# Row-count pairs in the score items, and four TensorE steps moved within the slot, in an attention and expert kernel

## The reference, cut to what matters

```
xn  = layernorm(x)                                  # no scale, no shift
q, k, v = xn Wq^T + bq, xn Wk^T + bk, xn Wv^T + bv  # 16 heads of 8
attn    = softmax(causal(q k^T / sqrt(8))) v  Wo^T + bo
logits  = xn gate^T                                 # 8 experts
moe     = sum over the best 2 experts of softmax(top 2 logits) * (xn We[e])
out     = x + attn + moe
```

## Time and profile before

| | |
|---|---|
| median of three runs | 512.64 us |
| the profiled execution's own time | 513.41 us |
| its span, first to last instruction | 511.3 us |
| PE busy (TensorE matmul) | 476.1 us, 93% |
| DVE busy (VectorE) | 420.2 us, 82% |
| ACT busy (ScalarE) | 395.3 us, 77% |
| POOL busy (GpSimd) | 346.7 us, 68% |
| mean granted TensorE clock | 0.98 of full speed |

### The profile page before, as it was taken

How to read it: one execution, slowest core, us unless ns; L and a number is a source line. 1 busy time by engine, 2 the same in 40 slices (tenths; PEclk the granted TensorE clock), 3 DMA queues, 4 the chain that set the end, 5 groups by cost and what they waited for, 6 DMA issues and landing times.

```text
span 511.3 us, 17283 instructions
## 1 busy us (share of the span) xinstructions
PE 476.1 (93%) x6242; PEld 390.2 (76%) x6242; DVE 420.2 (82%) x1144; ACT 395.3 (77%) x1063; POOL 346.7 (68%) x561
## 2 busy tenths in 40 slices
PE   2548799999999999999999999999999999999985
PEld 1426588888888888888888888888888888888863
DVE  5898688888888988888888988888888988887721
ACT  3545578888888888888888888888888888887773
POOL 7264747777777777777777777777777777755443
PEclk9967989999999999999999999999999999999998
DMA  4755755556555666655555565655555566551000
GB/s 124 193 141 121 182 122 149 148 136 148 134 139 140 145 164 151 146 144 143 133 140 140 144 163 144 157 142 144 135 135 140 143 163 152 131 140 38 14 13 22
DMA packets 64345, 67.78 MB, mean 133 GB/s; under 512 B 7916, under 2 KB 59244, under 8 KB 59548
## 3 DMA queue, kind: packets, MB, share of 16 engines
q1 hardware_dynamic: 64260, 66.68, 52.5%
HBM read 44.90 MB, written 21.23 MB: 129 GB/s over the span
## 4 chain that ended last, share of the span: by engine, by line
PE 85%; issue 4%; DMA 3%; POOL 3%; ACT 2%; DVE 2%; SPq 0%; POOLq 0%; DVEq 0%; ACTq 0%
PE m L856 22%; PE oT_ps L926 17%; PE scoreT_ps L902 12%; PE score_ps L882 11%; PE scoreT_ps L907 5%; PE score_ps L876 5%; PE m L968 3%; PE m L1011 3%; PE m L1029 3%; PE m L941 2%; PE m L1036 1%; DMA scratch<-parts 1%; DMA qstack<-mT 1%; ACT probs L502 1%; POOL parts L374 1%
## 5 line engine op out<-in xcount | busy, mean ns | idle before, releaser
L630 DVE TENSOR_REDUCE negmax<-score_ps 128x2 f32<-128x512 f32 (+1 forms) x384 | 250.6, 680 | 56.7 <-PE score_ps L882 52.7
L502 ACT ACTIVATE probs<-scoreT_ps 128x512 f32<-128x512 f32 x384 | 216.8, 603 | 75.5 <-PE scoreT_ps L902 48.0
L397 POOL TENSOR_TENSOR fours<-lower,upper 128x512 f32<-128x512 f32 x64 | 81.7, 1276 | 54.0 <-ACT upper L552 54.0
L856 PE MATMUL m<-we_hl,xnT_hl 128*128 128x512 f32 x384 | 113.6, 417 | 0.0
L882 PE MATMUL score_ps<-kstack,qstack 72*128 72x128 bf16 (+1 forms) x1024 | 103.4, 223 | 6.0 <-DVE negmax L630 5.8
L902 PE MATMUL scoreT_ps<-qstack,kstack 123*128 123x128 bf16 (+1 forms) x1024 | 101.8, 221 | 4.2 <-DMA qstack<-mT 3.5
L926 PE MATMUL oT_ps<-probs,vaug 128*32 128x256 f32 (+1 forms) x2048 | 97.3, 330 | 0.2 <-ACT probs L502 0.2
L902 PEld LDWEIGHTS scoreT_ps<-qstack,kstack 123*128 123x128 bf16 (+1 forms) x1024 | 67.9, 98 | 27.3 <-ACT probs L502 15.3
L926 PEld LDWEIGHTS oT_ps<-probs,vaug 128*32 128x32 f32 x2048 | 57.4, 110 | 29.3 <-ACT probs L502 0.4
L552 ACT ACTIVATE upper<-m,weight 128x128 f32<-128x128 f32 x256 | 73.3, 377 | 8.1 <-PE m L856 8.1
L882 PEld LDWEIGHTS score_ps<-kstack,qstack 72*128 72x128 bf16 (+1 forms) x1024 | 71.9, 100 | 9.1 <-DVE negmax L630 8.6
(11 more groups left out here) (84 smaller groups left out, 641.0 us busy)
## 6 DMA issues: line engine op xcount, KB each, us to landing
kstack<-scratch SPq DMA_DIRECT2D x93, 192.0 KB
scratch<-parts SPq DMA_DIRECT2D x64, 192.0 KB, 2.3
qstack<-scratch SPq DMA_DIRECT2D x62, 192.0 KB
qstack<-scratch SPq DMA_DIRECT2D x31, 256.0 KB
x_sb<-in_x SPq DMA_DIRECT2D x32, 128.0 KB, 2.3
scratch<-parts SPq DMA_DIRECT2D x32, 128.0 KB, 1.9
out<-out_sb SPq DMA_DIRECT2D x32, 128.0 KB, 2.9
kstack<-scratch SPq DMA_DIRECT2D x6, 96.0 KB
```

What stands on the lines that cost most here:

```text
L397: g.tensor_tensor(fours[:, :, q, :], lower[:, :, q, :], upper[:, :, q, :], ALU.add).then_inc(pool_sum, 1)
L502: a.activation(o, i, ACT.Exp, scale=SCALE).then_inc(act_exp, 1)
L630: v.tensor_reduce(o, score_ps[n % 2][:].rearrange("p (h k) -> p h k", h=w), axis=AX.X, op=ALU.max, negate=True).then_inc(dve_max, 1)
L856: ins = tn.matmul(o, l, r, start=first, stop=l is low)
```

## The change

The results are the same, and the number of matmuls, copies and reductions is the same.

- **Row-count pairs.** Within a score item of 72 and 123 rows, and a transposed one of 123 and 74, the two matmuls with few rows are issued first, then the two with 123.
- **Maxima.** Their transpose goes behind the projection in step 1 and into `oT_ps` rather than m0; the products with the values of step 3 wait for the copy `mT`.
- **Expert product 2** (the third of four) moves from step 9 to step 8, right behind the turned attention output. VectorE's `o_sb` moves ahead of the maximum of step 9.
- **Normalised values** are turned in step 11 rather than 10, behind the turned input. The copy `oTn` on ScalarE follows it.
- **Output product** with Wo, VectorE's `out_sb` and the store move to step 1 of the next slot.

```diff
@@ score_item
-                    for c in range(2):
-                        h = head(grp, 2 * (j - 1) + c)
-                        for q, top in ((0, MAX_ROW), (1, ALL_ROWS)):
+                    for q, top in ((0, MAX_ROW), (1, ALL_ROWS)):
+                        for c in range(2):
+                            h = head(grp, 2 * (j - 1) + c)
                             ins = tn.matmul(ps[:, c * S + q * P:c * S + (q + 1) * P], qs[0:top, h, P:S],
@@ scoreT_item
-                    for c in range(2):
-                        h = head(grp, 2 * j + c)
-                        for q, top in ((0, ALL_ROWS), (1, MAX_ROW + MAX_PARTS)):
+                    for q, top in ((1, MAX_ROW + MAX_PARTS), (0, ALL_ROWS)):
+                        for c in range(2):
+                            h = head(grp, 2 * j + c)
@@ TensorE, slot
+                    if n == 1 and has(s, -3):
+                        give_output(t + (-3))
...
+                    if n == 1 and has(s, PRE):
+                        pe.wait_ge(act_upper, upto(fin, per=2))
+                        project(pre)
                     if n == 1 and has(s, -1):
                         pe.wait_ge(dve_split, upto(mix, per=2))
-                        pe.wait_ge(dve_out, upto(fin + (-1)))
-                        tn.transpose(m0[:, 0:P // 2].bitcast(BF16), ...
-                    if n == 1 and has(s, PRE):
-                        pe.wait_ge(act_upper, upto(fin, per=2))
-                        project(pre)
+                        pe.wait_ge(act_oT, upto(fin + (-1)))
+                        tn.transpose(oT_ps[:, 0:P // 2].bitcast(BF16), ...
                     if n == 3 and has(s, -2):
+                        if has(s, -1):
+                            pe.wait_ge(act_mT, upto(mix))
                         values(fin, 0)
                         values(fin, 1)
...
                     if n == 8 and has(s, -2):
                         pe.wait_ge(act_oT, upto(fin))
-                        if has(s, -1):
-                            pe.wait_ge(act_mT, upto(mix))
-                        else:
-                            pe.wait_ge(dve_out, upto(fin + (-1)))
+                        pe.wait_ge(dve_out, upto(fin + (-1)))
...
-                    if n == 9 and has(s, -1):
+                    if n == 8 and has(s, -1):
                         pe.wait_ge(dve_lower, upto(mix, per=2, k=1))
                         experts(mix, 2)
...
                         turn_input(t + NXT)
+                    if n == 11 and has(s, -2):
+                        pe.wait_ge(dve_o, upto(fin))
+                        for q in range(QT):
+                            ins = tn.transpose(m0[:, q * P:(q + 1) * P], o_sb[:, q, :], ident[:])
+                        ins.then_inc(pe_oTn, 1)
                     if n == 11 and has(s, -1):
                         pe.wait_ge(act_upper, upto(mix, per=2, k=1))
                         experts(mix, 3)
@@ VectorE, slot
                     if n == 1 and has(s, NXT):
                         measure(t + NXT)
+                    if n == 1 and has(s, -3):
+                        add_output(t + (-3))
...
                         ins.then_inc(dve_den, 1)
-                    if n == 9 and has(s, -2):
-
                         dve.wait_ge(dve_den, upto(fin))
                         dve.wait_ge(pe_oTn, upto(fin + (-1)))
@@ ScalarE, slot
                     if n == 11 and has(s, NXT):
                         copy_input(t + NXT)
+                    if n == 11 and has(s, -2):
+                        act.wait_ge(pe_oTn, upto(fin))
+                        act.wait_ge(pe_y, upto(fin + (-1)))
+                        a.copy(oTn[:], m0[:, 0:S]).then_inc(act_oTn, 1)
```

More of the change, by code:

```diff
@@ L313, in slot @@
             def slot(t, s):
-                if has(s, -3):
-                    store(t + (-3))
                 if has(s, -1):
@@ L323, in slot @@
                     load_stacks(Seq(0, PRE), slice(0, H), dma_stack[PRE])
+                if has(s, -3):
+                    store(t + (-3))
                 if has(s, NB):
@@ L563, in slot @@
                         act.wait_ge(dma_max, upto(mix + (-1), unit=16))
-                        a.copy(mT[:], m0[0:MAX_PARTS * QT * H, 0:P // 2].bitcast(BF16)).then_inc(act_mT, 1)
+                        a.copy(mT[:], oT_ps[0:MAX_PARTS * QT * H, 0:P // 2].bitcast(BF16)).then_inc(act_mT, 1)
                     if n == 2 and has(s, PRE):
@@ L592, in slot @@
                         upper_experts(mix, 0)
[L593 to L596, removed]
             act.wait_ge(pool_const, 2)
@@ L725, in fill_stack, with add_output @@
                               steps[HALF:P].unsqueeze(1).to_broadcast([HALF, H * QT, P])).then_inc(dve_stack, 1)
+            def add_output(m):
+                dve.wait_ge(pe_y, upto(m))
+                dve.wait_ge(pool_sum, upto(m, per=RESULT))
+                dve.wait_ge(dma_out, upto(m + (-1), unit=16))
+                v.tensor_tensor(out_sb[:].rearrange("p q d -> p (q d)"), m0[:, 0:S],
+                                res[:].rearrange("p q d -> p (q d)"), ALU.add).then_inc(dve_out, 1)
             def take_rest(pre):
@@ L782, in slot @@
                         split_max(t)
[L783 to L788, removed]
+                    if n == 11 and s == NSEQ + 1:
+                        add_output(fin)
             def first_normalised(nxt):
@@ L951, in project, with give_output @@
                 ins.then_inc(pe_qk, 1)
+            def give_output(m):
+                pe.wait_ge(act_oTn, upto(m))
+                for q in range(QT):
+                    ins = tn.matmul(m0[:, q * P:(q + 1) * P], oTn[:, q * P:(q + 1) * P], wo_sb[:], start=True, stop=True)
+                ins.then_inc(pe_y, 1)
             def slot(t, s):
@@ L1003, in slot @@
                         pe.wait_ge(act_oT, upto(fin))
-                        if has(s, -1):
-                            pe.wait_ge(act_mT, upto(mix))
-                        else:
-                            pe.wait_ge(dve_out, upto(fin + (-1)))
+                        if s == 2:
+                            pe.wait_ge(dve_bias, 1)
+                        pe.wait_ge(dve_out, upto(fin + (-1)))
                         for q in range(QT):
@@ L1022, in slot @@
                         turn_input(t + NXT)
-                    if n == 11 and has(s, -1):
-                        pe.wait_ge(act_upper, upto(mix, per=2, k=1))
-                        experts(mix, 3)
                     if n == 11 and has(s, -2):
[L1027 to L1033, removed]
                         pe.wait_ge(dve_o, upto(fin))
@@ L1037, in slot @@
                         ins.then_inc(pe_oTn, 1)
+                    if n == 11 and has(s, -1):
+                        pe.wait_ge(act_upper, upto(mix, per=2, k=1))
+                        experts(mix, 3)
+                    if n == 11 and s == NSEQ + 1:
+                        give_output(fin)
+                    if f:
+                        scoreT_item(f, k)
             pe.wait_ge(pool_const, 5)
```

5 lines of the change are left out of this document (2 added, 3 removed).

## The result

The changed kernel takes **523.28 us** (median of 4 runs, 522.16 to 524.85) against 513.02 us for the kernel before (4 runs, 511.35 to 516.01): ratio 1.0199, 95% interval 1.0163 to 1.0235. It is slower. The profiled execution, the slowest of its four, took 524.85 us with a span of 522.7; the one of before took 513.41 with 511.3.

A forecast was written before the change was run, and what follows sets the result against it. TensorE's list, with no slack behind VectorE's `lower`, was taken to bound the kernel. 27 slots at 0.35 us give +9.5, less 0.8 in slots 29 to 31: 522.1 from the profiled 513.41, 521.3 against the median; range 515 to 525.

The forecast's parts named there:

- no slack from `lower` to line 941: Line 941's load waits 0.05 us for VectorE's `lower`; whatever makes `lower` later lengthens the slot.
- Part A: From line 1011's first matmul to the turned input's weight load (line 941, now 944): 3.14 us, 0.33 more than now.
- The stop on TensorE: TensorE stands 0.7 us in all, before score item 11 (0.3) and before line 944's load (0.4).
- Part B: Rest of the slot: normalised values +0.22, output product net 0, projection -0.13, pairs -0.07, neighbours +0.01; +0.03 us.
- Pairs: Score items: 28 fewer row-count changes per slot, three costing 0.01 us, save 0.09, of which 0.07 in Part B.
- rival 3: Pairs save nothing, row counts being in one tiling mode: +0.07 per slot in Part B, 523 us, chance 0.08.
- Covers: Delays stay hidden: line 545 before the projection's load by 0.13 us, `mT` before the products with the values by 0.5.
- rival 4: The projection also waits for line 545: 0.08 us more per slot, 523.5 us, chance 0.07.
- Rivals 1 and 2: TensorE's savings come through, 503 us, chance 0.11; or the stop is half as long, 517 us, chance 0.08.
- rival 1: If `lower`, done ahead of maximum 9, were in time for line 944, 0.34 us saved per slot; 503 us, chance 0.11.
- slots 29 to 31 turn no input, so no wait stands there and TensorE only saves: Last slots, without line 944: each gets 0.2 to 0.3 us shorter, -0.8 us in all.
- slot 1 hides it in slot 2's wait: Slot 1's added time vanishes in slot 2's 3.51 us wait for a DMA, so only 27 slots count.

The follow-up runs named there:

- e1: Changed kernel with expert product 2 back in step 9, `o_sb` left ahead of maximum 9; 519.54 us, ratio 1.0126 to the kernel before.
- e4: Changed kernel with product 2 back in step 9 and VectorE doing maximum 9, `lower`, then `o_sb`; 513.35 us, ratio 0.9997 to the kernel before.
- e8: Changed kernel with the row-count pairs undone; 526.63 us, ratio 1.0284 to the kernel before.
- e5: Kernel before with the row-count pairs alone; 510.21 us, ratio 0.9966 to the kernel before.
- e3: Changed kernel with product 2 back in step 9 and `o_sb` back behind maximum 9; 514.51 us, ratio 1.0026 to the kernel before.
- e7: Changed kernel with the maxima turned ahead of the projection in slot 1 alone; 523.62 us, ratio 1.0225 to the kernel before.
- e6: Kernel before with the pairs, and the maxima turned behind the projection into `oT_ps` except in slot 1; 505.3 us, ratio 0.9875.
- e2: Changed kernel with `o_sb` back behind maximum 9, product 2 left in step 8; 533.26 us, ratio 1.0394 to the kernel before.

## Why the prediction was right, and where it was not

The forecast of 521.3 us, slower by 1.7%, stands against 523.28; the mechanism is the one it gave.

- **TensorE bound, no slack from `lower` to line 941.** Right. In every kernel run here the load of the turned input comes 0.05 us after `lower` ends, and A follows `lower` alone: e1 to e4 move it from 2.59 to 3.49.
- **Part A, +0.33.** Measured +0.34. The terms one by one: line 1022 and product 1.15 (275.52 - 274.37; predicted 1.14), transposed item 0.24, score item 0.38, 0.04 to the maximum, 0.61 to `lower` (0.60), 0.68, 0.05. Score item 9 ended 1.77 after line 1022's start, to the hundredth. Had 0.55 been taken for the maximum, as behind `rden`, the sum would have been 0.06 short.
- **The stop on TensorE, 0.7, in two gaps of 0.3 and 0.4.** Right: 0.27 and 0.36.
- **Part B, +0.03.** Measured +0.03. Four 4-byte transposes and the product take 278.73 - 277.52 = 1.21 where the earlier trace rows had 0.97, so +0.24 for the normalised values (predicted 0.22). The output product takes 0.50 (280.14 - 279.64), +0.05 as predicted. Lines 979 to 990 take 281.38 - 280.14 = 1.24 where the earlier trace rows had 260.84 - 259.42 = 1.42: -0.18, exactly the 0.05 + 0.13 that the steps gave.
- **Pairs, -0.09, of which -0.07 in B.** Measured -0.10, all of it in B (e8). The page on TensorEngine Tiling in the Trainium skill (Key Properties) puts the drain at a change of mode; it says nothing of changes within one mode, and the prediction took that for a saving of nothing in rival 3. e8 (+0.10 per slot) and e5 (ratio below 1 in its whole interval) show a saving, so rival 3 falls here, though not by much.
- **Covers.** The projection did not wait for line 545. ScalarE's line 545 ended at 280.35, and the projection's weights loaded with the last matmul of line 979, as the sum had it; this is the load and the cast:

```profile
280.49 0.66 PEld L859 LDWEIGHTS m<-xnT_hl,wqk_hl 128*128 128x128 f32 x5
```

```profile
279.93 0.42 ACT L545 CAST xnT_hl<-xnT_high 128x256 fp32r<-128x256 f32 x1
```

  0.14 of cover, predicted 0.13: rival 4 falls. `mT` ended at 281.84 and the products with the values started at 282.38: 0.5 of cover, as forecast.
- **Per slot +0.35, slot 14.7.** Measured +0.36, 14.73. Rivals 1 and 2 fall with it. e4 also shows what stands behind rival 1's condition: with `lower` ahead of `o_sb` and the product back, `o_sb` is next in line and the gain stops at 0.1 per slot.

**What was mis-sized are the ends.** The span grew by 11.4 us; the sum had 8.65 for it. These are single executions, the changed kernel's being 1.6 us above its median; by the medians the loss is 10.3 us. So some of what follows on start and end may be what two executions of one kernel differ by. The turned-back attention output (line 1011, now 1022) cuts the difference in four, by the rows of both kernels. Before:

```profile
81.60 0.60 PE L1011 MATMUL m<-ident,oT 128*128 128x128 f32 x4
...
441.14 0.60 PE L1011 MATMUL m<-ident,oT 128*128 128x128 f32 x4
455.54 0.60 PE L1011 MATMUL m<-ident,oT 128*128 128x128 f32 x4
468.88 0.60 PE L1011 MATMUL m<-ident,oT 128*128 128x128 f32 x4
```

Changed:

```profile
82.83 0.61 PE L1022 MATMUL m<-ident,oT 128*128 128x128 f32 x4
...
451.17 0.61 PE L1022 MATMUL m<-ident,oT 128*128 128x128 f32 x4
465.90 0.61 PE L1022 MATMUL m<-ident,oT 128*128 128x128 f32 x4
479.30 0.61 PE L1022 MATMUL m<-ident,oT 128*128 128x128 f32 x4
```

| stretch | before | changed | more | the sum had |
|---|---|---|---|---|
| to slot 3's row | 81.60 | 82.83 | +1.23 | +0.35 |
| 25 slots | 359.54 | 368.34 | +8.80 | +8.75 |
| slot 28 to 29 | 14.40 | 14.73 | +0.33 | +0.35 |
| from there to the end | 55.76 | 56.80 | +1.04 | -0.8 |

The steady part is right to 0.05 us in 8.8. The step that failed is "slots 29 to 31 turn no input, so no wait stands there and TensorE only saves". They lose line 944's wait, but not the other half of the stop: score item 11 still waits for maximum 9, which still waits for score item 9 behind the product. In slot 29 of the changed kernel two items take 0.72 again, where two without a wait take 0.45:

```profile
467.74 0.39 PE L885 MATMUL score_ps<-kstack,qstack 72*128 72x128 bf16 x4
...
468.46 0.40 PE L885 MATMUL score_ps<-kstack,qstack 72*128 72x128 bf16 x4
```

Slot 29 to 30 takes 13.40 against 13.34, where the sum had 13.1 or so; e3, with neither the product nor `o_sb` moved, has 13.17. e1, with the product back, takes 476.06 - 462.82 = 13.24 and 55.2 from its row of 462.82 to its end, 1.6 less than the changed kernel. The last slots, in which TensorE waits for ScalarE, are part of it (12.64 and 10.72 against 12.50 and 10.26 in e1), and 0.8 of the 1.6 is the granted clock of the last six matmuls (last section). The other 0.8 is what the product's place costs the tail.

The start is the other half, +0.9 over the sum. There "slot 1 hides it in slot 2's wait" took the end of that wait as fixed, and it came 0.87 later. The DMA that ends it was issued 1.05 later (56.86 against 55.81), so the later issue is a reason that fits; but e7, which issued it early again, had most of the delay all the same. Executions differ here: e1, whose slots are shorter, reaches slot 3's row at 83.50, later than the changed kernel's 82.83. No run settles the cause.

## What to carry to other kernels

Before moving work ahead on the engine that is the bound, follow who consumes what is pushed back: here the product's move costs 0.66 us a slot by itself, and 0.33 with `o_sb` moved too, because score item 9 feeds a VectorE that works in order and whose chain ends at the bound engine's next load. Judge each part of a bundle by itself: two parts of this change are worth 1.2% (e6), and the others cost more than that, 0.25 us a slot in part B, above all by taking two transposes out of the stretch whose length VectorE sets, and 0.33 by making that stretch longer. A wait can be real without a bracket in the timeline; compare distances from start to start with the same instructions elsewhere.

## What the runs showed of the hardware that was not expected

- Behind `rden` (0.35 us long) the maximum, which doesn't need its result, starts 0.26 us after it; `o_sb`, which reads it and waits for its semaphore, starts 0.38 after it (e1). So the order costs 0.12 us here without any change in work. Whether the reading or the semaphore makes the difference, no run separates.
- A change of row count (72 or 74 and 123) between bf16 matmuls of 128 columns costs 3 to 4 ns, and the time shows one matmul behind the change: 60, 55, 59, 55 ns in an item of 72, 72, 123, 123 rows, 59.5, 58, 58, 58 in one of 72, 123, 72, 123 (changed, e8).
- The granted clock (1.00 is 2.4 GHz, 0.50 is 1.2, and a figure between is a stretch with both) differs between executions after the long wait of slot 2. From 63.5 to 66 us it is 0.52 in the changed kernel, whose wait was 3.56 us; in e5, whose wait was 1.76, it is 1.00. The others: before 3.51 us of wait and 0.63, e1 3.50 and 0.50, e3 3.44 and 0.73, e7 3.86 and 0.50, e8 3.19 and 0.68; e2 3.05 and 1.00, e4 2.75 and 1.00, e6 2.13 and 1.00. In these ten executions the six longest waits are followed by a clock below 1.00 and the other four are not, though among the six the order isn't strict. Where it is so, a late DMA is paid for once more.
- The same at the very end. The last output product (four 4-byte matmuls), in the windows view, columns as in the earlier trace rows, of the changed kernel, of the kernel before and of e1:

```profile
518.70:520.00 1.30, 1.22 (x4) 0.93 (x4) 0.00 (x0) 0.03 (x1) 0.00 (x0) 0.50 0.00 0
```

```profile
507.50:508.60 1.10, 0.99 (x4) 0.70 (x4) 0.00 (x0) 0.03 (x1) 0.00 (x0) 0.67 0.00 0
```

```profile
514.50:515.30 0.80, 0.71 (x4) 0.52 (x4) 0.02 (x1) 0.00 (x0) 0.00 (x0) 1.00 0.00 0
```

  The same work takes 1.22, 0.99 and 0.71 us at 0.50, 0.67 and 1.00. The Trainium skill (TensorE: Matmul & The Clock Gate, Part 1) has a gate between half and full clock, set by how busy the engine has lately been; these stretches follow waits of the engine (0.91 and 0.46 us in the changed kernel's last slot), which fits; but e1 waited as long there and has 1.00. Line 1037's last two matmuls, just ahead, take 0.69 in the changed kernel and 0.44 before. Together 0.48 us of the changed kernel's loss at its end is this; that the change is the cause of it, no run here shows.
